# Sixteen blocks instead of thirteen fetched row by row, and a late projection of 1000 nodes instead of 500

## The reference

```
h     = relu(layernorm(x))                         # per node
h0    = edge_attr @ W0 + b0                        # per edge, 32 -> 64
g     = gelu(gelu(h0) @ W1 + b1) @ W2 + b2
score = (h0 + g) @ W3 + b3                         # per edge, 64
msg   = h[src] * score
wV    = segment_sum(msg, dst) / max(count, 1)      # per node
out   = x + wV @ Wo + bo
```

## Time and profile before

| | us |
|---|---|
| median of 3 runs | 3926.53 (3926.48 to 3933.37) |
| profiled execution | 3928.06 |
| its span | 3926.3 |
| POOL busy | 2948.4 |
| PE busy | 3063.5 |
| DVE busy | 1299.3 |
| ACT busy | 850.0 |

### The profile page before, as it was taken

One profiled execution on the slowest core, in us unless ns is written; L12 is line 12 of the kernel. 1 busy time (PEld: TensorE's weight loads), 2 busy tenths in 40 slices (PEclk: granted clock), 3 DMA queues, 4 the chain that ended last, 5 costly groups with the idle time before them and its releaser, 6 DMA issues.

```text
span 3926.3 us, 55941 instructions
## 1 busy us (share of the span) xinstructions
PE 3063.5 (78%) x8729; PEld 1466.1 (37%) x8730; DVE 1299.3 (33%) x2572; ACT 850.0 (22%) x1241; POOL 2948.4 (75%) x3125
## 2 busy tenths in 40 slices
PE   3886878777778778778877778788778777778778
PEld 1443333333333333333333333333333333333345
DVE  7333323333223333223333223333223333223334
ACT  4222212122222222222122212122222122222111
POOL 7777777777777777777777777777777777777775
PEclk9888778778777778778778777777777778778767
DMA  6122221111111111111111111111111111111112
GB/s 161 42 44 44 44 43 42 41 41 42 41 41 41 44 39 44 39 44 41 41 41 41 41 41 41 43 42 39 44 41 41 41 41 41 41 41 41 44 35 58
DMA packets 164649, 176.52 MB, mean 45 GB/s; under 512 B 86257, under 2 KB 86386, under 8 KB 163984
## 3 DMA queue, kind: packets, MB, share of 16 engines
q0 software_dynamic: 99808, 102.40, 13.7%
q1 hardware_dynamic: 53112, 67.00, 6.0%
q10 hardware_dynamic: 11432, 4.61, 0.4%
HBM read 167.34 MB, written 6.40 MB: 44 GB/s over the span
## 4 chain that ended last, share of the span: by engine, by line
POOL 61%; issue 21%; PE 11%; SPq 2%; DMA 2%; DVE 1%; ACTq 1%; ACT 0%; DVEq 0%; POOLq 0%
POOL rows L414 61%; DMA rows<-h_rows,idx 2%; SPq L367 2%; PE ps_wb L613 1%; PE ps_wa L613 1%; PE ps_h1a L593 1%; PE ps_h1a L590 1%; PE ps_h1b L583 1%; PE ps_h1b L593 1%; PE ps_sb L602 1%; ACTq L542 1%; PE ps_h1b L590 1%; PE ps_sa L602 1%; PE ps_h1a L583 1%; PE ps_h0b L574 1%
## 5 line engine op out<-in xcount | busy, mean ns | idle before, releaser
L414 POOL DMA_INDIRECT rows<-h_rows,idx x3071 | 2902.4, 945 | 937.0 <-issue 924.5
L613 PE MATMUL ps_wb<-ln_sq,msg 128*128 128x128 f32 x1608 | 324.0, 364 | 447.8 <-DVE acc L970 437.5
L844 DVE TENSOR_TENSOR msg<-ps_sb,rows 128x512 f32<-128x512 f32 x194 | 133.9, 690 | 1162.2 <-DMA rows<-h_rows,idx 1162.2
L844 DVE TENSOR_TENSOR msg<-ps_sa,rows 128x512 f32<-128x512 f32 x196 | 135.3, 691 | 1142.5 <-DMA rows<-h_rows,idx 1142.5
L613 PE MATMUL ps_wa<-ln_sq,msg 128*128 128x128 f32 x1616 | 289.5, 334 | 284.5 <-DVE acc L970 278.3
L613 PEld LDWEIGHTS ps_wb<-ln_sq,msg 128*128 128x128 f32 x1608 | 275.7, 259 | 611.3 <-DVE acc L970 563.7
L964 DVE TENSOR_REDUCE hot_sum<-ln_sq 128x64 f32<-128x512 f32 x403 | 415.1, 1030 | 13.3
L613 PEld LDWEIGHTS ps_wa<-ln_sq,msg 128*128 128x128 f32 x1616 | 245.1, 232 | 443.6 <-DVE acc L970 398.0
L486 ACT ACTIVATE score_t<-ps_h1a,b_last 128x512 f32<-128x512 f32 x202 | 138.9, 688 | 1094.5 <-PE ps_h1a L593 974.9
L486 ACT ACTIVATE score_t<-ps_h1b,b_last 128x512 f32<-128x512 f32 x201 | 138.2, 687 | 894.6 <-PE ps_h1b L593 767.8
L590 PE MATMUL ps_h1a<-attr,w_attr 64*128 64x512 f32 x404 | 319.3, 881 | 0.0
(11 more groups left out here) (102 smaller groups left out, 2096.4 us busy)
## 6 DMA issues: line engine op xcount, KB each, us to landing
ln_sq<-h_rows SPq DMA_DIRECT2D x7904, 0.2 KB
ln_sq<-h_rows ACTq DMA_DIRECT2D x5408, 0.2 KB
attr<-in_edges SPq DMA_DIRECT2D x201, 256.0 KB
rows<-h_rows,idx POOLq DMA_INDIRECT x3071, 2.6
xs<-in_x SPq DMA_DIRECT2D x4, 700.0 KB
h_rows<-ln_d ACTq DMA_DIRECT2D x4, 700.0 KB
dst_i<-in_dst SPq DMA_DIRECT2D x1, 1612.0 KB, 26.9
rows<-in_dst_rows SPq DMA_DIRECT2D x4, 384.0 KB
```

What stands on the lines that cost most here:

```text
L414: pool.indirect_dma_start(rows[:, slot, t, :], None, table, bass.IndirectOffsetOnAxis(ap=idx[:, s, t:t + 1], axis=0),).then_inc(gathered[s ...
L613: pe.matmul(window[0:m * D, 0:m * WIN], msg[:, s % 2, t:t + m, :].rearrange("p t d -> p (t d)"), hot[:, k, t:t + m, :].rearrange("p t n -> ...
L844: dve.tensor_tensor(msg[:, s % 2, 0:n, :], ps_s[s % 2][:, 0:n * D].rearrange("p (t d) -> p t d", d=D), near, ALU.mult).then_inc(msg_done, 1)
```

## The change

Sixteen blocks are spare: 23 and every 25th after it (23, 48, ... 398). POOL gathers 387 blocks in place of 390. SP fetches 18 parts of each (576 rows in place of 608), ACT's queue 14 parts (448 rows in place of 416). SP's pace is 24 rows per block in place of 20, ACT's 18 in place of 14 (two times 9 in place of two times 7).

The late projection takes 1000 nodes in two groups of four tiles, one per PSUM bank, with two `output` calls; SP waits for both and writes all in one DMA. So `N_EARLY` is 11500, `EARLY_BLOCKS` 375 in place of 391, and the early projection has groups of 115 in place of 120 partitions; it comes after step 377.

```diff
-LATE_TILES = 4
+LATE_PER = 4
+LATE_GROUPS = 2
+LATE_TILES = LATE_PER * LATE_GROUPS
-PERIOD = 31
+PERIOD = 25
-SP_PARTS = 19
-SP_ROWS = 20
-ACT_ROWS = 7
+SP_PARTS = 18
+SP_ROWS = 24
+ACT_ROWS = 9
...
-            sp.wait_ge(y_ready, len(groups) + 1)
+            sp.wait_ge(y_ready, len(groups) + LATE_GROUPS)
...
             def project_late():
 
-                for t in range(LATE_TILES):
-                    at = N_EARLY + t * NP
-                    mm = pe.matmul(ps_h1[0][0:NP, t * DC:(t + 1) * DC], acc[:, at:at + NP], wo,
-                                   start=(t == 0), stop=(t == LATE_TILES - 1), skip_group_check=True)
-                mm.then_inc(proj_done, 1)
+                for half in range(LATE_GROUPS):
+                    for t in range(LATE_PER):
+                        at = N_EARLY + (half * LATE_PER + t) * NP
+                        mm = pe.matmul(ps_h1[half][0:NP, t * DC:(t + 1) * DC], acc[:, at:at + NP], wo,
+                                       start=(t == 0), stop=(t == LATE_PER - 1), skip_group_check=True)
+                    mm.then_inc(proj_done, 1)
...
             def output_late():
-                output(len(groups), ps_h1[0], LATE_TILES, NP, y_late[:, :, :], x_late[:, :, :])
+                for half in range(LATE_GROUPS):
+                    tiles = slice(half * LATE_PER, (half + 1) * LATE_PER)
+                    output(len(groups) + half, ps_h1[half], LATE_PER, NP, y_late[:, tiles, :], x_late[:, tiles, :])
```

## The result

| | before | after |
|---|---|---|
| median of 4 runs, us | 3926.51 (3925.52 to 3933.37) | 4005.98 (4002.7 to 4007.5) |
| ratio, 95% interval | | 1.0201 [1.0189, 1.0213] |
| profiled span, us | 3926.3 | 4000.9 |
| message of block 402, us | 3916.2 | 3987.4 |
| mean granted clock of PE | 0.788 | 0.791 |

The change makes the kernel 2.0% slower. The profiled span is 75 us longer than before, where I had forecast 50; the median is 79 us longer, 6 us above the top of my range. The profiled execution was the fastest of the four, 3 us under their median; no trace shows what made the others longer. (Behind the edits, L414 became L416, L361 L363, L367 L369, L311 L313, L537 L539, L542 L544, L574 L576, L602 L604, L486 L488, L651 L653, L844 L847.)

A forecast was written before the change was run, and what follows sets the result against it. POOL was taken to bound the kernel before, giving 3926.3 - 30.0 - 12.0 + 1.7 = 3886 us alone; with SP, projection and ACT setting the pace, message 402 at 3964 plus tail 10.1 + 1.7 gave 3976 us, range 3932 to 4000.

The forecast's parts named there:

- SP takes over from POOL: Steady part: SP needs 9.78 us per block against POOL's 9.59, so SP sets the pace from near block 175.
- Rival A: Whole run: POOL keeps the pace, faster, and the kernel takes 3886 us; chance 0.08.
- SP at iteration 371: SP's queue before the early projection: 279 parts at 12.74 us and 185 loads bring it there at 3713 us.
- Rival B: SP's queue and the projection: SP binds only in part, or the pause is half hidden; 3887 to 3940 us, chance 0.10.
- Projection with POOL without a lead: Early projection: PE's pause of 46.0 us becomes POOL's, costing 45 of 82 us lost; score 377 at 3786 us.
- Catching up at ACT's pace: After the projection: ACT's 18 rows per block set 7.6 us per block, where PE alone needs 5.8.
- rival C: The end: ACT does not set the pace, POOL ends it; 3968 us, chance 0.14.
- rival D: Catching up: PE does not return to the full clock, 8.0 us per block; 3985 to 4000 us, chance 0.15.
- From `keep_score(395)` on: Last blocks: ACT's pace holds, `keep_score(399)` at 3946.5 us, 167 us after `keep_score(377)`; message 402 at 3964.
- Tail: After the last message: 10.1 us as before plus 1.7 for the late projection of 1000 nodes.

The follow-up runs named there:

- Shorter parts: Changed kernel with the last 4 of 32 row DMAs of each SP part left out, 28 issued; ratio 0.9907 to the kernel before, span 3888.1 us.
- pace 23: Changed kernel with SP fetching 23 rows per block in place of 24; 3932.0 us against 3932.93 for the kernel before.
- the spare blocks alone: Changed kernel with the late projection of before, 500 nodes, output on 120 partitions; 4026.47 us against 3925.64 for the kernel before.
- The held-back output: Changed kernel with early output DMAs cut into 112 and 3 partitions and issued once block 400 is scored; ratio 1.017 to the kernel before.

## Why the prediction was right in kind and wrong in size

By its own steps, spans against 3976:

- **SP takes over from POOL.** Right, but sooner: forecast near block 175, first hole at block 133. Shorter parts and pace 23, each by itself, gave POOL its pace back. Rival A falls.
- **SP at iteration 371.** Forecast 3713, measured 3719.9: +7 us. My sum took 12.74 us per part; SP waited 0.4 us in all on the way, so from 75.1 to 3719.9 the same sum gives (3719.9 - 75.1 - 185 x 0.45) / 279 = 12.765 us. 0.025 us by 279 parts is the term's error. Rival B, which needed 12.60, was on the wrong side.
- **Projection with POOL without a lead.** Right: 44.3 us in place of 46.0, POOL's hole 38.4 us in place of 45, all of it ended by the score. Score 377 at 3793 in place of 3786. POOL lost 90 us on scores where I said 82: 51 by SP's pace (forecast 37) and 38 by the projection (forecast 45). The last gathers differ by as much, 3961.1 here and 3871.5 in the kernel with short parts.
- **Catching up at ACT's pace.** Right until 3925: `keep_score(377)` at 3786.2 and `(395)` at 3925.3 are 139.1 / 18 = 7.73 us per block (forecast 7.6), +2 us by then. That ACT held the pace shows in the chain from 3794 to 3926 us, by line:

```profile
by line: ACTq L544 54.3%; ACTq L539 15.3%; issue 13.3%; ACT score_t L488 2.7%; PE ps_h1a L595 2.3%; PE ps_h1a L592 2.3%; PE ps_h1b L585 2.0%; PE ps_h1b L595 1.5%; PE ps_h1b L592 1.5%; PE ps_h1a L585 1.3%; ACT g L482 1.0%; PE ps_sb L604 1.0%
```

ACT's queue has 70% of it, so rival C falls. PE's granted clock had a mean of 0.85 from 3786 to 3926, between the full clock that I took and the mix of rival D; no line of PE has more than 2.3% of that chain.
- **From `keep_score(395)` on: the step that failed.** I took "`keep_score(399)` 22 x 7.6 = 167 us later" for a stretch in which I had not looked at what SP does. Behind the last edge load SP issues the early output, at 3929.37 (at 3880.05 before). Before, that was after ACT's last row; with 18 rows per block, and the last spare block at 398 near the end, it falls into ACT's rows. Cost: 31.2 us in place of 15.2 for two blocks, +16 us. The late projection of 1000 nodes also made it 115 partitions in place of 120; by the run with the spare blocks alone (24.6 us) about 7 of the 16 us are of that, and the rest would have come with 120 too. The held-back output took the stall away (16.0 us), though message 402 came only 10.9 us sooner: that kernel was 2.8 us later already at `keep_score(395)` (3928.1). From there to message 402 it took 48.4 us against 62.1, so the output's worth at the end is about 14 us.
- **Tail.** 13.5 us in place of 11.8: +1.7. The second `output` took what I had for it; the DMA of twice the size was waited for 4.2 us in place of 2.3, where I had bounded the growth at 1 us and taken 0.4 without a row to show it.

The sum: +7 for SP's parts, +2 for ACT's pace, +16 for the output and +1.7 for the tail make 27; the last messages came about 2 us closer than I had them, which leaves the 25 by which the profiled span is longer than forecast; the median is 5 us above that span, 2 us of time outside it and 3 us by which this execution was the faster one, and no trace shows what those 3 are. All but the output's term is read from one execution.

Most of the miss is one omission. I listed what the change adds and moves; the output DMAs were neither, but the edit moved ACT's rows beside them.

## What to carry to other kernels

When rows or loads are taken off a full engine and given to DMA queues, add up each queue's issue time per block and compare it with the pace that is wanted; what stands behind them in the queue (here the edge loads) pays, although the DMA engines are busy at a share of only 0.2. Then go through the last stretch and ask which large DMAs run beside the queue that will set the pace there. And spread the fetched blocks so that none is due near the end.

## What the runs showed that I had not expected

**Partitions and DMA engines.** The output on 115 partitions ran at a share of 0.40 to 0.46 with 141 to 159 GB/s, on 120 partitions at up to 0.99 with 273, on 112 + 3 at up to 0.99 with 322. The Trainium skill, DMA: Bandwidth & Descriptors, section Why a DMA increments its semaphore by 16 and not by 1, says that a DMA runs on as many of the 16 engines as the largest number up to 16 that divides the slowest dimension of both its sides. By that, 115 partitions get 5 engines, 120 get 15, 112 get 16. The shares agree with an estimate from it: 5/16 = 0.31, and the gathers beside it, at 0.14 in the stretch ahead, make 0.45.

**A queue that only issues small DMAs slows down beside a large one.** ACT's issue of a row took 0.23 us, and 0.5 to 1.5 us in the chain while the output ran; the register load took 7.81 us in place of 2.3 ahead of it. The Trainium skill states, in the same section of DMA: Bandwidth & Descriptors, that the queue uses the lowest-numbered engines for a DMA on fewer than 16. If so, a row DMA would always meet such an output there; that is my inference, and no run here shows which engine a row took. Few engines are not the whole cause: on 120 partitions nine rows took 15.48 us, on 112 + 3 they took 12.04, and only the time that the output ran was shorter.
